# Attention on one core: constant products ahead of three steps of the scores

## What is computed

```
x = x + 0.5 * ffn(layernorm(x))
x = x + attn(layernorm(x))          # 16 heads of 16, rotary, causal
x = x + 0.5 * ffn(layernorm(x))
x = x + 0.5 * moe(layernorm(x))     # 16 experts, top 2, and a shared one
x = x + mamba(layernorm(x))
x = x + 0.5 * moe(layernorm(x))

# attn:
Q, K, V = proj(Wq, bq), proj(Wk, bk), proj(Wv, bv)      # 16 heads
Q, K = rope(Q), rope(K)
scores = where(causal, Q @ K.T / 4, -inf)
out = (softmax(scores) @ V) @ Wo.T + bo
```

## Time and profile before

| | |
|---|---|
| median of three runs | 860.14 us |
| profiled execution, its own time | 868.81 us |
| its span, first to last instruction | 867.6 us |
| mean granted TensorE clock over the span | 0.909 |
| TensorE busy | 730.7 us (84%) |
| VectorE busy | 603.1 us (70%) |
| ScalarE busy | 375.6 us (43%) |
| GpSimd busy | 361.8 us (42%) |

### The profile page before, as it was taken

One profiled execution on the slowest core, in us unless ns is written; L12 is line 12 of the kernel. 1 busy time (PEld: TensorE's weight loads), 2 busy tenths in 40 slices (PEclk: granted clock), 3 DMA queues, 4 the chain that ended last, 5 costly groups with the idle time before them and its releaser, 6 DMA issues. The chain is left out here.

```text
span 867.6 us, 11766 instructions
## 1 busy us (share of the span) xinstructions
PE 730.7 (84%) x3803; PEld 480.5 (55%) x3803; DVE 603.1 (70%) x1060; ACT 375.6 (43%) x756; POOL 361.8 (42%) x436
## 2 busy tenths in 40 slices
PE   3978799789999898889948969987969979898990
PEld 2766555344433476568825645654536645466880
DVE  6987644666661387756438898888999999984333
ACT  4321233335556343413304765687646645331330
POOL 4344122212011332524631037774858868361562
PEclk9989667789887999989979989998999999998995
DMA  4946623013366150146540000000006000023535
GB/s 184 320 55 89 99 37 49 6 26 105 107 198 198 51 242 30 63 125 186 162 151 1 0 1 1 1 1 1 1 13 279 0 1 2 30 87 94 158 113 181
DMA packets 46637, 74.75 MB, mean 86 GB/s; under 512 B 8258, under 2 KB 36674, under 8 KB 45010
## 3 DMA queue, kind: packets, MB, share of 16 engines
q1 hardware_dynamic: 42066, 61.61, 25.4%
q0 software_dynamic: 4512, 12.39, 4.0%
HBM read 35.45 MB, written 30.47 MB: 76 GB/s over the span
## 5 line engine op out<-in xcount | busy, mean ns | idle before, releaser
L1319 PE MATMUL PS<-FB,C 128*128 128x512 f32 x256 | 129.4, 610 | 3.5 <-DVE FB L2017 3.5
L1424 ACT ACTIVATE FA<-PS 128x512 f32<-128x512 f32 (+3 forms) x192 | 80.7, 496 | 71.2 <-PE PS L1065 70.7
L2124 POOL DMA_INDIRECT GY<-FB x62 | 61.1, 986 | 76.0 <-DVE FB L1905 47.5
L2096 POOL TENSOR_SCALAR_AFFINE_SELECT FA<-FA 128x128 f32<-128x128 f32 x128 | 36.3, 295 | 130.7 <-ACT FA L1424 128.5
L1715 DVE TENSOR_REDUCE FA<-PS 128x2 f32<-128x1024 f32 (+2 forms) x64 | 67.8, 1086 | 18.1 <-PE PS L1044 17.8
L2148 POOL TENSOR_TENSOR FB<-FB,RBF 128x512 f32<-128x512 f32 x51 | 66.0, 1295 | 30.0 <-DVE FB L2008 29.9
L929 PE MATMUL PS<-TRI 128*128 128x512 bf16 x201 | 54.1, 414 | 14.3 <-DMA FB<-GY 12.0
L1065 PE MATMUL PS<-RA 64*128 64x512 f32 (+3 forms) x192 | 60.0, 501 | 5.0 <-ACT FA L1424 5.0
L1200 PE MATMUL PS<-WE,FB 128*128 x248 | 63.6, 402 | 0.6 <-ACT FB L1463 0.6
L1319 PEld LDWEIGHTS PS<-FB,C 128*128 128x128 f32 x256 | 46.9, 197 | 28.3 <-issue 20.1
L1065 PEld LDWEIGHTS PS<-RA 64*128 64x128 f32 x192 | 29.3, 223 | 52.3 <-ACT FA L1424 31.0
(11 more groups left out here) (282 smaller groups left out, 1646.5 us busy)
## 6 DMA issues: line engine op xcount, KB each, us to landing
GX<-ZT SPq DMA_DIRECT2D x4, 4160.0 KB, 15.0
WE<-in_wr SPq DMA_DIRECT2D x8, 1536.0 KB, 10.8
FB<-GX SPq DMA_DIRECT2D x62, 130.0 KB, 2.2
RA<-RA SPq DMA_DIRECT2D x48, 128.0 KB, 4.8
FB<-GY SPq DMA_DIRECT2D x8, 512.0 KB, 5.6
FA<-in_w SPq DMA_DIRECT2D x2, 1024.0 KB, 7.1
FA<-in_qkvo SPq DMA_DIRECT2D x1, 1536.0 KB, 19.6
FB<-in_we SPq DMA_DIRECT2D x4, 384.0 KB, 3.6
```

What stands on the lines that cost most here:

```text
L1319: pe.matmul(bank(m), ident, shc[k % 4], start=n == 0, stop=n == DN - 1).then_inc(*yad.inc(ch, n, m))
L1424: act.activation(PT[n % 12][:, c0:], bank(ring_bank[(x, *a)])[:, c0:], ACT.Exp, scale=0.25).then_inc(*exd.inc(*a))
L2124: pool.indirect_dma_start(GY, bass.IndirectOffsetOnAxis(ap=ids[:, b:b + 1], axis=0), yout[pi % 4][:, (b - b0) * D:(b - b0) * D + D], None) ...
```

## The change

A helper `warm(here, n)` is added. It looks up the next step, from this one on, that uses the ring of three banks, waits as that step will for its bank to be free, and issues `n` constant products into it. The next user of the bank overwrites them. It is called at three places of each of the eight pairs of chunk and group: four products ahead of the second `diag` (`i` = 2), three ahead of the first `off` of `i` = 2, and three ahead of the last `pv`. That is 80 products. Nothing is taken away and nothing else is moved.

```diff
+            def warm(here, n):
+
+                use = next(y for y in plan[plan.index(here):] if y in ring_bank)
+                busy(claim_ring(use), n)
+
...
                 elif x in ("diag", "off"):
                     ch, g, i, *h0 = a
+                    if i == 2 and h0 in ([], [0]):
+                        warm((x, *a), 4 - len(h0))
                     bk = claim_pair(x, *a)
...
                         pe.wait_ge(*vad.at(ch if kt >= ch * TC else 0, kt % TC // 2))
+                    if kt == ch * TC + TC - 1:
+                        warm((x, *a), 3)
                     pe.wait_ge(*exd.at(ch, g, kt, 3))
```

## The result

Twenty runs of the changed kernel had a median of 855.57 us (851.55 to 860.75), and twenty of the kernel before, in the same rounds, 861.81 us (855.26 to 867.45). The ratio is 0.994, with a 95% interval of 0.9917 to 0.9964. The change made the kernel faster by 0.6%, some 5 to 6 us. I had forecast 13. The sign was right and the time lies inside the range, but the gain is less than half of the forecast one. The ratios in this document leave out runs that took over 1.5% more than the fastest of the same kernel, most of them runs at a low clock, while the medians hold all runs, so that a ratio and the medians beside it can disagree by up to 0.002.

What follows compares the result with a forecast made beforehand. TensorE was taken to bound attention, with 81 us of it at half clock. Products cost 8 us and 61 us at 0.35 give back 21, so 8 - 21 = -13 us, 847 us from the median; range 834 to 862.

Steps and rivals of the forecast that it cites:

- The mechanism: In attention, products put into the stretches with TensorE waits that precede the nine clock falls would hold the clock up.
- How much of the 81 us goes: Of 81 us at half clock in attention, three quarters, 61 us, would go; bounds 27 and 81 us.
- the same 13 us off the median: The 13 us gain worked out on the profiled execution was taken off the runs' median, 860.14 us, giving 847 us.
- The give-back per microsecond: In attention, each microsecond at half clock removed would give back 0.35 us; bounds 0.21 and 0.47.
- The products' price: The 80 products in attention would cost 8 us, most of their 17.2 us lying in waits; bounds 2 and 17.
- the 7.2 us: Products' cost outside waits: 1.9 us ahead of second diagonals, 3.9 ahead of `off`, 1.4 ahead of the last `pv`.
- three products ahead of `off`: Ahead of the `off` of `i` = 2, three would cost 0.645 us in each of six groups, 3.9 us in all.
- the four and three others: Four ahead of the second `diag`, 0.46 us at waits of 0.40; three ahead of the last `pv`, 0.645 without a wait.
- The new wait: Each `warm` waits earlier for an exponential that the next `sc` needs anyway; costed at nothing.
- the falls move: Rival: falls shift to other attention stretches, only a third of the 81 us goes, 860 us; chance 0.12.
- the clock falls as before: Rival: the products in attention are only a burden, 14 us slower at 874 us; chance 0.11.

Runs made afterwards that it cites:

- e0_before: The kernel before, unchanged, run again beside the other versions: median 870.77 us, ratio 0.999 against before in the same rounds.
- e6_waits: The changed kernel with the early waits for the bank kept and no products issued: median 871.35 us, ratio 1.0008 against the kernel before.
- e9_look: The kernel before, unchanged, in one more profiled execution: 857.72 us, with 44 us at half clock within attention.
- e5_double: The changed kernel with twice the products at each place (eight, six and six): median 876.50 us, ratio 1.0071 against the kernel before.

## Why the prediction was off by half

**The mechanism** was right in its first half: the products keep the clock up. It went from 0.921 to 0.946, from 0.932 to 0.952 and from 0.927 to 0.945 in three sets, and the parts each move it. That this pays more than it costs holds for the medians and for the execution that I read (202.6 to 191.0 us of attention), and is not seen against the four profiled executions of before with 44 to 48 us.

**The step that failed** is "How much of the 81 us goes", and behind it "the same 13 us off the median". The share that I took, three quarters, was near for that execution: 81 us before and 13.6 after, with 14 to 20 in the three other profiles of the changed kernel. But the 81 us belonged to one execution, and I took them off the median of others. Timed runs give the difference as 2 x (0.9455 - 0.921) x 870 = 43, 2 x 0.020 x 858 = 34 and 2 x 0.0175 x 866 = 30 us over the whole span, in place of 61. The sign of it was in the prediction's own text: the profiled execution lay 8.7 us above the median. At 0.35 us per us these are 25 us more at half clock than in an ordinary run; 81 - 25 = 56, three quarters of it 42, times 0.35 less 8 is 7 us, or 853 us.

**The give-back per microsecond**, 0.35, was somewhat high. The clean pair of groups gives 0.32, the group before it at least 0.37. The two kinds of execution give (202.6 - 192.2) / (81 - 44) = 0.28. Over 34 of the 35 runs of before in the first set (one at 0.878 left out), a line through time and clock falls by 5.7 us per 0.01 of clock, that is per 17.4 us at half clock, 0.32; in the other three sets it is 0.29, 0.25 and 0.28. The page of the Trainium skill "TensorE: Matmul & The Clock Gate" (section Terms) prices it at 0.50, and none of these values agrees with that. The likely reason is that the other engines are a floor, as the rows of before had shown.

**The products' price**, 8 us, was near or somewhat high. The one group that can be compared directly at full clock paid 0.70 us instead of 1.1, and eight times that would be 5.6; but the group before it paid at least 1.3. By the runs, the changed kernel lies 7.7, 6.3 and 5.6 us above each set's own line of before at equal clock. How the 7.2 us are made up is less sure: three products ahead of `off` cost 0.12 us in two groups, where I had 0.645, while the four and three others cost 1.3 in one of them, where I had 0.46 + 0.645. A likely reason for the low price of the first group is that a wait of 0.22 us for an exponential ahead of an `sc` soon after, seen in `e0_before`, is gone after the change. With terms from the middle of what was measured, 35 us at 0.32 less 6 is 5 us, what the result shows; at 0.28 and 7 it would be 3, so the runs do not fix the terms more closely than that.

**The new wait** cost nothing that the runs can tell, as said: `e6_waits` is at 1.0008 (0.9976 to 1.0039).

**The rivals.** That the falls move, so that a third of the time at half clock goes and the time stays, happened in part: more than a third went in every profile of the changed kernel, but new falls came near 128 us, and its 860 us is about as near to the result as my 847. That the clock falls as before did not happen. The section of the same page of the Trainium skill that asks for no long idle gaps ("Why this matters for your kernels") does not agree with these traces: TensorE's longest wait in the attention of the earlier trace rows is 1.55 us and the clock fell nine times, and products in waits of 0.4 to 1.1 us held it up.

**What stays open.** Which executions of before the gain of the medians comes from, since no trace shows one between 48 and 81 us at half clock in attention. Whether the fall pattern of an execution is set by where the program's start lies against something that runs on its own was not tried. That `e0_before` and `e9_look` have their falls in attention at the same places to 0.1 us, and the execution of the earlier trace rows at quite others, speaks for it.

## What to carry to other kernels

Before a forecast is made from one profiled execution, its own time should be set beside the median of the runs, and the difference explained: here 8.7 us were the clock's luck, and a gain that consists of taking this luck away is overstated by most of that. Where runs carry their mean clock, time against clock gives the price of a microsecond at half clock from the kernel itself. A higher clock is not yet a shorter time: here 24 to 31 us less at half clock gave back about what 80 products cost. Products that fill a wait are cheap until the wait is full (0.70 us for ten in one group, at least 1.3 in another), and cost nearly their full length after that (2.0 us for the next ten).

## What the runs showed of the hardware

The granted clock of one program differs between its executions: 0.907 to 0.931 in 34 of 35 runs of the kernel before on one chip, with times of 863.69 to 881.01 us. In its six profiled executions the time at half clock within attention was 44, 44, 44, 48, 81 and 90 us. A run of 128x512 constant products in bf16 starts one every 0.215 us at full clock, also when it is six (1.47 us) or eight long (1.90 us, both in `e5_double`): (1.90 - 0.39) / 7 = 0.216.
